# Turning every second tile of the first pass with VectorE and a DRAM round trip instead of TensorE

## The reference

```
x = x + s4(cond(x, style))         # first pass
x = x + ffn(cond2(x, style))       # second pass
cond:  four modulated 1-D convolutions (same, upsample, same, downsample), no nonlinearity between them
s4:    y = causal convolution of each row with one 1024-long kernel K, plus D * u
ffn:   base linear 1024 -> 1024, plus a routed LoRA (8 experts, top 2, rank 16)
```

## Time and profile before

| | |
|---|---|
| median of 3 runs | 1319.42 us (1319.32 to 1320.6) |
| profiled execution: time, span | 1320.42 us, 1318.6 us |
| TensorE busy | 1276.2 us (97%) |
| VectorE, GpSimd, ScalarE busy | 1043.9 (79%), 916.6 (70%), 842.3 us (64%) |
| DMA moved | 158.23 MB, mean 120 GB/s |
| first pass, turns 1 to 32 | 68.38 to 590.88 us of the span |
| a first-pass turn without extra work | 15.5 us |

### The profile page before, as it was taken

One profiled execution on the slowest core, in us unless ns is written; L12 is line 12 of the kernel. 1 busy time (PEld: TensorE's weight loads), 2 busy tenths in 40 slices (PEclk: granted clock), 3 DMA queues, 4 the chain that ended last, 5 costly groups with the idle time before them and its releaser, 6 DMA issues.

```text
span 1318.6 us, 23280 instructions
## 1 busy us (share of the span) xinstructions
PE 1276.2 (97%) x8214; PEld 1220.5 (93%) x8214; DVE 1043.9 (79%) x2311; ACT 842.3 (64%) x1772; POOL 916.6 (70%) x730
## 2 busy tenths in 40 slices
PE   3789999999999999999999999999999999999999
PEld 3578899999899999999999999999999999999998
DVE  7777878777877777877878888788887878788872
ACT  4577777778777877776556555565656565565640
POOL 6458888666666777666768766676776767676752
PEclk9789999999999999999999999999999999999999
DMA  3234455445544554455443342433425252433433
GB/s 131 78 92 138 124 142 150 133 122 146 134 135 135 137 136 138 131 151 147 85 130 105 101 134 79 126 109 111 124 83 152 79 149 86 131 104 114 121 85 90
DMA packets 86278, 158.23 MB, mean 120 GB/s; under 512 B 26634, under 2 KB 48403, under 8 KB 86035
## 3 DMA queue, kind: packets, MB, share of 16 engines
q1 hardware_dynamic: 84898, 154.79, 41.8%
q10 hardware_dynamic: 1264, 1.96, 0.5%
HBM read 93.79 MB, written 33.56 MB: 97 GB/s over the span
## 4 chain that ended last, share of the span: by engine, by line
PE 87%; DVE 5%; POOL 4%; ACT 2%; issue 1%; DMA 1%; SPq 0%; POOLq 0%; DVEq 0%; ACTq 0%
PE psum L1905 28%; PE psum L1907 28%; PE psum L1906 27%; PE psum L2036 2%; POOL xs_l L964 1%; DMA w3T<-in_w_dram 1%; POOL vs_l L959 1%; POOL as_l L993 1%; PE psum L289 1%; DVE vm_l L1635 0%; POOL vbuf L943 0%; POOL vbuf L939 0%; DVE turned L1685 0%; DVE a_l L1662 0%; PE psum L2203 0%
## 5 line engine op out<-in xcount | busy, mean ns | idle before, releaser
L1905 PE MATMUL psum<-wt_h,u_h 128*128 128x386 f32 (+1 forms) x760 | 261.2, 344 | 0.0
L1907 PE MATMUL psum<-wt_h,u_l 128*128 128x386 f32 (+1 forms) x760 | 258.3, 340 | 0.0
L1906 PE MATMUL psum<-wt_l,u_h 128*128 128x386 f32 (+1 forms) x760 | 258.0, 340 | 0.0
L939 POOL TENSOR_TENSOR vbuf<-vbuf 128x512 f32<-128x512 f32 x64 | 97.7, 1526 | 170.4 <-ACT vbuf L1260 170.4
L1685 DVE STREAM_TRANSPOSE turned<-vbuf 32x256 f32<-32x256 f32 x480 | 208.9, 435 | 7.9 <-ACT vbuf L1246 0.7
L953 POOL TENSOR_TENSOR vm_f<-vm_f 128x512 f32<-128x512 f32 x64 | 82.8, 1293 | 120.8 <-DVE vm_l L1635 120.4
L1253 ACT ACTIVATE vbuf<-psum,tabs 128x512 f32<-128x512 f32 x128 | 105.2, 822 | 93.2 <-PE psum L1907 89.6
L1905 PE MATMUL psum<-a_h,vm_h 128*128 128x256 f32 x512 | 148.4, 290 | 3.2 <-ACT vbuf L1253 3.0
L1906 PE MATMUL psum<-a_l,vm_h 128*128 128x256 f32 x512 | 146.0, 285 | 0.0
L1907 PE MATMUL psum<-a_h,vm_l 128*128 128x256 f32 x512 | 145.8, 285 | 0.0
L1905 PEld LDWEIGHTS psum<-wt_h,u_h 128*128 128x128 f32 x760 | 143.7, 189 | 0.5
(11 more groups left out here) (336 smaller groups left out, 4187.5 us busy)
## 6 DMA issues: line engine op xcount, KB each, us to landing
vm_f<-vv SPq DMA_DIRECT2D x256, 112.0 KB, 4.3
xin<-in_x_ph_dram SPq DMA_DIRECT2D x32, 512.0 KB, 5.0
xr<-in_x_row_dram SPq DMA_DIRECT2D x32, 512.0 KB, 3.9
x1d<-xr SPq DMA_DIRECT2D x64, 256.0 KB, 3.3
xin<-x1d SPq DMA_DIRECT2D x32, 512.0 KB, 4.0
xr<-x1d SPq DMA_DIRECT2D x64, 256.0 KB, 5.2
xo<-in_b_base_dram SPq DMA_DIRECT2D x32, 512.0 KB, 5.6
out_dram<-xo SPq DMA_DIRECT2D x31, 512.0 KB, 2.8
```

Source lines behind the costliest of these rows:

```text
L939: G.tensor_tensor(v3[:, :, 1:H:2], v3[:, :, 1:H:2], by_odd, ALU.subtract).then_inc(v3_odd, 1)
L1905: nc.tensor.matmul(to, stat_h, mov_h, start=first_ and n == 0, stop=False, skip_group_check=True)
L1906: nc.tensor.matmul(to, stat_h, mov_l, start=False, stop=False, skip_group_check=True)
L1907: ins = nc.tensor.matmul(to, stat_l, mov_h, start=False, stop=end, skip_group_check=True)
```

## The change

It concerns the tiles g = 3, 5, ... 31 of the first pass ("spun" tiles, 15 of them).

- TensorE no longer turns them. VectorE does two 32x32-block transposes of the finished tile into `xo` (`spin`, after `layer0(i+1)` and before `composed2(i+1)` in turn i), having written the corrected end columns itself. SyncE, at the head of its list of turn i+1, stores `xo` to a DRAM tensor `spin`, waits until it has landed and until `s4` of the tile before is done, and loads it back with four DMAs so that the blocks change places.
- In turn i+1 ScalarE makes `u_h` from `xo` in two halves after `third_evacuated` and before `layer0`, and `s_h` after `layer0`. VectorE makes the neighbour sums and the low part of one half before its `layer0`. GpSimd makes the low part of the other half and `s_l`, after `combined` (`landed`).
- In turn i+1 TensorE runs `step1` before `s4`. `s4` of a spun tile waits for both halves of the low part before its tail, and its order is tail, phases, both. `layer0(i+1)` doesn't wait for the turned tile there.
- The residual additions follow the new order, with `composed1` between them. The high part of the first weights `y1_h` moves in these turns from VectorE to ScalarE.

```diff
+            def spin(g):                                   # SyncE
+                sp.wait_ge(tr_done, at(g))
+                sp.dma_start(sh.spin, xo[:, :]).then_inc(spin_out, 16)
+                sp.wait_ge(spin_out, 16 * spins(g))
+                sp.wait_ge(s4_done, at(g - 1))
+                for t in range(4):
+                    src = bass.AP(tensor=sh.spin.tensor, offset=sh.spin.offset + 2 * P * t, ap=[[L, 32], [32 * L, 4], [1, 2 * P]])
+                    sp.dma_start(xo[32 * t:32 * t + 32, :].rearrange("p (f n) -> p f n", f=4), src).then_inc(u_land, 16)
             def body(i):
+                if spun(i - 1):
+                    spin(i - 1)
                 if first(i - 2):
...
+            def landed(g):                                 # GpSimd
+                pool.wait_ge(u_hi, at(g))
+                G.tensor_tensor(u_spun[1][:, 1], u_runs[:, 1], u_spun[0][:, 1].bitcast(F32), ALU.subtract).then_inc(odd_lo, 1)
+                pool.wait_ge(s_hi, at(g))
+                G.tensor_tensor(s_spun[1], s_runs, s_spun[0].bitcast(F32), ALU.subtract).then_inc(s_lo, 1)
...
-                if first(i - 1):
+                if first(i - 1) and not spun(i - 1):
                     sum_low(i - 1)
                 if here(i):
                     combined(i)
+                if spun(i - 1):
+                    landed(i - 1)
...
+            def landed(g):                                 # ScalarE
+                act.wait_ge(u_land, 64 * spins(g))
+                for q in range(2):
+                    ins = A(u_spun[0][:, q], u_runs[:, q], ACT.Copy)
+                ins.then_inc(u_hi, 1)
...
+                elif spun(i - 1):
+                    if here(i):
+                        act.wait_ge(tr_done, at(i - 1))
+                        pair_evacuated(i, 0)
+                    if here(i + 2):
+                        scaled1(i + 2)
...
+            def landed(g):                                 # VectorE
+                ve.wait_ge(u_land, 64 * spins(g))
+                ve.wait_ge(s_lo, at(g - 1))
+                V.tensor_tensor(s_runs, u_runs[:, 0, :, 0:6], u_runs[:, 1, :, 0:6], ALU.add).then_inc(sum_ready, 1)
+                ve.wait_ge(u_hi, at(g))
+                V.tensor_tensor(u_spun[1][:, 0], u_runs[:, 0], u_spun[0][:, 0].bitcast(F32), ALU.subtract).then_inc(u_lo, 1)
+            def spin(g):                                   # VectorE
+                c, t = place(g)
+                ve.wait_ge(v3_val, at(g))
...
+                V.tensor_copy(v3[:, :, 0:H:H - 1], sh.vfix[:, c, batches(t), :]).then_inc(v3_fix, 1)
+                ve.wait_ge(v3_fix, at(g))
+                ve.wait_ge(s_lo, at(g - 1))
+                for b in range(2):
+                    ins = V.transpose(view(xo, 32 * b, (256, 4), (64, 4), (1, 32)),
+                                      v3[:, b, :].rearrange("p (n t x) -> p t n x", t=4, x=32))
+                ins.then_inc(tr_done, 1)
...
                 if here(i + 1):
                     layer0(i + 1)
+                if spun(i):
+                    spin(i)
...
                     residual_begin(i - 1)
-                    if crowded(i) and here(i + 2):
+                    if (crowded(i) or spun(i - 1)) and here(i + 2):
                         composed1(i + 2)
                     residual_end(i - 1)
...
+                if spun(g):                                # TensorE, s4
+                    pe.wait_ge(u_lo, at(g))
+                    pe.wait_ge(odd_lo, spins(g))
+                product(ps_tail, [(*s4_rows(g, 7 - r), sh.tail_h[:, r, :, :].rearrange("p q n -> p (q n)"),
...
+                for to, stat, tb in ((*phases, both) if spun(g) else (both, *phases)):
+                    if stat is None:
+                        pe.wait_ge(s_lo, at(g))
...
+                if spun(i - 1) and here(i + 2):
+                    pe.wait_ge(blur, at(i + 1))
+                    step1(i + 2)
                 if first(i - 1):
...
-                if here(i) and not by_blocks(i):
+                if here(i) and not by_blocks(i) and not spun(i):
                     if here(i + 1):
                         pe.wait_ge(a_lo, at(i + 1, 2, 1))
                         pe.wait_ge(as_sum, at(i + 1))
```

More of the change, by code:

```diff
@@ L158, in build @@
         sh.kpad = nc.dram_tensor("kpad", [1, PAD + L], F32, kind="Internal").ap()
+        sh.spin = nc.dram_tensor("spin", [P, L], F32, kind="Internal").ap()
         sh.x1d = nc.dram_tensor("x1d", [TILES, P, 2, H], F32, kind="Internal").ap()
@@ L438, in program @@
     u_l = sb("u_l", [P, KT, 2, C], FR)
+    u_spun = [view(t, 0, (512, 2), (32, 2), (64, 8), (1, 32)) for t in (u_h, u_l)]
     vm_f = sb("vm_f", [P, 2, 2, 2, P])
@@ L459, in program @@
     s_h = sb("s_h", [P, 3, P], FR)
+    with ExitStack() as landing:
+        s_in = sb("s_in", [P, 3 * P], F32, landing)
     s_l = sb("s_l", [P, 3, P], FR)
@@ L471, in program @@
     hw = sb("hw", [P, ER])
+    s_spun = [view(t, 0, (32, 2), (64, 6), (1, 32)) for t in (s_h, s_l)]
+    s_runs = view(s_in, 0, (32, 2), (64, 6), (1, 32))
+    u_runs = view(xo, 0, (512, 2), (256, 2), (32, 8), (1, 32))
     hwT_h, hwT_l = s_h[:, 0, :], s_h[:, 1, :]
@@ L576, in program @@
     in_scaled = sem("in_scaled")
+    spin_out, u_land, odd_lo = sem("spin_out"), sem("u_land"), sem("odd_lo")
     ms_sum, ms_hi, ms_lo = sem("ms_sum"), sem("ms_hi"), sem("ms_lo")
@@ L695, in nth, with spun, spins @@
         return n * (g - HALVED) + i + 1
+    def spun(g):
+        return here(g) and SPUN <= g < TILES and (g - SPUN) % 2 == 0
+    def spins(g):
+        return max(0, (g - SPUN) // 2 + 1)
     def turned_f(g):
@@ L820, in body @@
                 if turn_is(i, TILES):
+                    sp.wait_ge(u_lo, TILES)
+                    sp.wait_ge(odd_lo, spins(TILES - 1))
                     sp.wait_ge(s_lo, TILES)
@@ L1602, in scaled1 @@
                 c, t = place(g)
-                if g > 2:
+                if g > 2 and not spun(g - 3):
                     if t == 0:
@@ L1838, in body @@
             def body(i):
-                if here(i - 1):
+                if here(i - 1) and not spun(i - 1):
                     turned(i - 1)
-                if first(i - 1):
+                if first(i - 1) and not spun(i - 1):
                     even_and_odd(i - 1)
@@ L1886, in body @@
                     lora(place(i - 1)[1])
-                if here(i + 2) and not (first(i - 1) and crowded(i)):
+                if here(i + 2) and not (first(i - 1) and (crowded(i) or spun(i - 1))):
                     composed1(i + 2)
@@ L2040, in rows, with s4_rows @@
                 return (u_h[:, k, :, :].rearrange("p b c -> p (b c)"), u_l[:, k, :, :].rearrange("p b c -> p (b c)"))
+            def s4_rows(g, k):
+                if spun(g):
+                    return [view(t, 512 * (k % 2) + P * (k // 2), (1, P)) for t in (u_h, u_l)]
+                return rows(k)
             def s4(g, i):
@@ L2047, in s4 @@
                     pe.wait_ge(toep_lo, 1)
-                product(ps_tail, [(*rows(7 - r), sh.tail_h[:, r, :, :].rearrange("p q n -> p (q n)"),
+                if spun(g):
+                    pe.wait_ge(u_lo, at(g))
+                    pe.wait_ge(odd_lo, spins(g))
+                product(ps_tail, [(*s4_rows(g, 7 - r), sh.tail_h[:, r, :, :].rearrange("p q n -> p (q n)"),
                                    sh.tail_l[:, r, :, :].rearrange("p q n -> p (q n)")) for r in range(2)], True, True)\
                     .then_inc(s4_tail, 1)
-                pe.wait_ge(s_lo, at(g))
                 if g == 0:
                     pe.wait_ge(toep_lo, 3)
-                for to, done, tb, stat in ((ps_p, s4_both, 0, None), (ps_q[:, 0, :], None, 1, 0), (ps_q[:, 1, :], s4_done, 2, 1)):
+                both = (ps_p, None, 0)
+                phases = ((ps_q[:, 0, :], 0, 1), (ps_q[:, 1, :], 1, 2))
+                for to, stat, tb in ((*phases, both) if spun(g) else (both, *phases)):
+                    if stat is None:
+                        pe.wait_ge(s_lo, at(g))
                     if stat == 1:
@@ L2057, in s4 @@
                     for j in range(3):
-                        st = (s_h[:, j, :], s_l[:, j, :]) if stat is None else rows(2 * j + stat)
+                        st = (s_h[:, j, :], s_l[:, j, :]) if stat is None else s4_rows(g, 2 * j + stat)
                         n = H - P * j
                         ins = product(to[:, P * j:H], [(*st, toep_h[:, tb, 0:n], toep_l[:, tb, 0:n])], j == 0, j == 2)
-                    if done is not None:
-                        ins.then_inc(done, 1)
+                    if stat == 1:
+                        ins.then_inc(s4_both if spun(g) else s4_done, 1)
+                    if stat is None:
+                        ins.then_inc(s4_done if spun(g) else s4_both, 1)
             def ffn(n, js=range(KT)):
@@ L2162, in body @@
                 if here(i + 1):
-                    if here(i - 1) and not by_blocks(i - 1):
+                    if here(i - 1) and not by_blocks(i - 1) and not spun(i - 1):
```

(2 more changed lines are left out.)

21 lines of the change are left out of this document (20 added, 1 removed).

## The result

The changed kernel takes 1403.61 us (median of 4 runs, 1402.75 to 1403.92), against 1319.37 (1317.98 to 1320.6) for the kernel before: a ratio of 1.0638 with a 95% interval of 1.0619 to 1.0656. It is 84.2 us slower. The profiled execution took 1403.92 us, with a span of 1402.1. The forecast was 1399, range 1367 to 1432.

What follows compares the result with a forecast made beforehand. TensorE, busy 97% of the span, was taken to set the first pass's time. Per pair -0.8 + 1.75 + 3.45 = +4.4 us, +66 for 15 pairs, -4 for small products, +18 for the clock: +80, 1399 us, range 1367 to 1432.

Steps and rivals of the forecast that it cites:

- The transposes, -0.8 per pair: TensorE loses eight transposes in the odd turn of each of 15 pairs of turns: 0.8 us gained.
- `spin` delays `c_l`: +1.75 per pair: VectorE's `spin` makes `c_l` late, so the next turn's `step2` waits 1.75 us (1.2 to 2.1).
- GpSimd's low part: +3.45 per pair: Odd half's low part stands behind `combined` on GpSimd, so `s4` of the spun tile waits 3.45 us (3.2 to 3.8).
- the six turns named: Turns 10, 12, 14, 20, 28, 30: small products between `third` and `s4` fill part of the gap, -4 us.
- The clock: +1.2 per B turn, 18 in all: TensorE's clock falls in most turns with the long waits: 1.2 us each (0 to 3), +18 us.
- B turn: Second turn of each of 15 pairs, where `s4` of the tile turned by VectorE runs; forecast 20.7 us or more.
- Rival 1: Both TensorE waits come, at `step2` and `s4`, but the clock stays up: 1381 us; chance 0.22.
- What was set at nothing: Costs taken as zero: SyncE's DRAM round trip, `s_l`, `vs_l`, and moved work of VectorE and ScalarE in idle time before `layer0`.
- rival 2: DRAM round trip ends last, +2 us per pair, 1429 us; chance 0.12, shared with two clock falls a turn.
- rival 3: Faster: TensorE's waits stay below the 0.8 us gained; if all fits, 12 us gained, 1307 us; chance 0.06.
- the 0.6 us of room before `step2`: VectorE's chain ends with `c_l` at 16.39 us, and the next turn's `step2` takes it at 16.99.
- Its signs: Expected in the profile: first-pass TensorE busy about 85%, 15 waits each near 1.7 and 3.4 us, lower clock after long waits.

Runs made afterwards that it cites:

- e2: Changed kernel with GpSimd making the low part of the odd half ahead of `combined`, `s_l` still behind it: 1376.16 us, ratio 1.0429.
- e1: Changed kernel with the moved `step1` issued six times instead of once, filling the wait before `s4` with useless products: 1387.16 us, ratio 1.0513.
- e5: Changed kernel with SyncE storing `xo` to DRAM and awaiting it twice before the loads: 1404.25 us, ratio 1.0648.
- e12: Changed kernel with the high part of the first weights moved back to VectorE: 1407.47 us over two runs.
- e6: Kernel before with seven of the eight TensorE transposes of the 15 tiles left out and nothing in their place: 1317.48 us, ratio 0.9988.
- e3: Changed kernel with VectorE making the low part of the odd half too, behind the even half, instead of GpSimd: 1365.03 us, ratio 1.0345.
- e7: Changed kernel with `composed1` before the last residual addition in odd turns, ScalarE's `u_h`, `s_h` and GpSimd's low parts brought forward: 1351.95 us, ratio 1.0248.
- e9: As e8, with ScalarE evacuating `pair(i, 0)` before copying the turned tile in odd turns: 1337.22 us, ratio 1.0131.
- e8: As e7, with `step1` before `s4` in odd turns as well and `composed1` made still earlier: 1332.39 us, ratio 1.011.

## Why the prediction was right

The forecast was 80 us on top, 84.2 were measured, and its terms came out as follows.

- **The transposes, -0.8 per pair.** A turn without extra work lasts 14.68 us, as forecast.
- **`spin` delays `c_l`: +1.75 per pair.** 1.38 in the undisturbed turn, 15.9 us in all instead of 26. The two transposes took 1.31 us, not 1.44, and the copy of the end columns 0.16, not 0.2. In turns 6, 14, 18 and 26 `composed1` stood earlier anyway and the wait was 0.2 us or less; these turns the sum had not set apart.
- **GpSimd's low part: +3.45 per pair.** 3.66, and 49.7 us in all. Small products filled part of it in the six turns named, in which the waits were 2.29 to 3.26 us; that is 5 us in sum where 4 were forecast. `e2` shows that the place in GpSimd's queue made 3.06 us of it.
- **The clock: +1.2 per B turn, 18 in all.** About 22 by `e1`. Rival 1, that it stays up, is refuted. Its rule was that of the Trainium skill, "TensorE: Matmul & The Clock Gate", Part 1: a window without matmuls brings the clock down. The trace agrees in that the falls come late in the long wait or just behind it, and never behind the 1.38 us one. But the length of the wait doesn't sort the turns. In 12 of the 15 B turns the clock fell; in turns 10, 12 and 14, with waits of 3.26, 2.83 and 2.43 us, it did not, and in 28 and 30, with 2.98 and 2.29, it did, for as long as in turn 24. Turn 6 has a fall of its own behind the 2.00 us wait for `xr` at its start; in `e1_filled` the same wait, 1.99 us, brought none. What sorts them is open. The forecast had read the rule as leaving the 3.45 us wait safe for the most part, and here the row of the kernel before was the better guide.
- **What was set at nothing.** The round trip is hidden (`e5`; 2.6 and 2.9 us for its DMAs), so the round trip of rival 2 is refuted. Its other half, two falls of the clock in a turn, happened once, in turn 6. `s_l` is hidden, and the move of the weights' high part is worth nothing (`e12`, in its waits). Not nothing were three waits for VectorE (`xr`, `ssq`, `xmid`), 6.1 us in all against 0.2 before, which no term had.

The sum, measured: -12.0 for the transposes, +15.3 and +49.7 for the waits, +22 for the clock, +5.9 for VectorE's other waits and -1.8 for fewer waits for `vs_l`, together +79.1. Some 5 us of the 84.4 are left. In `e1_filled`, at full clock, turn 24 lasts 20.96 us and its parts are 15.48 + 1.38 + 3.55 + 0.18 = 20.59; 0.37 us per B turn stay over, in steps of about 0.1 at each wait. The bracket before `step2` says 1.38 us, but `step2` starts 1.48 us late (2.99 us into the turn instead of 1.51), and its first product then takes 0.41 us where the earlier trace rows has 0.31. In 15 turns the 0.37 are 5.6 us.

Its signs were met too: over the first pass TensorE's busy share is 87% where about 85 was expected, and the B turns last 20.0 to 23.6 us.

So the total came out closer than its terms, and that was luck. `c_l` was priced 10 us too high in sum; the clock, VectorE's other waits and the restarts were 15 too low.

**The side statement that failed** is rival 3's gain of 15 x 0.8 = 12 us if both waits were gone. With no extra work on any engine, `e6` gains 1.6 us. TensorE's waits before, the 3.4 us of the earlier trace rows and 0.8 more, read as if it alone set the time, and the forecast wrote that what is taken off it counts; they don't say how soon the next engine follows. The forecast had noted the 0.6 us of room before `step2` for VectorE, but didn't take it off the gain. The expectations of `e3` and `e7` to `e9` repeated the mistake, crediting nearly the full wait, and that of `e2` allowed for one new wait only.

## What to carry to other kernels

Where all engines are about two thirds busy or more, as here, the gain of relieving the busiest is bounded by the slack of the next chain, so measure it first by leaving the work out, as `e6` does. An operation that feeds the next stage belongs in its engine's queue by its due time: placed behind 4.5 us of other work it made a 3.7 us wait. A wait of that length on TensorE cost more than itself here, by about 1.5 us of slow clock; where it can't be removed, useless products in it can give the clock back, as in `e1_filled`.

## What the runs showed of the hardware

- **Useless matmuls made the kernel faster.** 53 us of them gave back 16.4 (`e1`). In turn 24 the clock was at 1.2 GHz for some 3.4 us (0.87, 0.50 and 0.77 in three stretches of 2 us), in turns 4 and 20 for 6.8 us. Which turns fall, and for how long, differs between the traces of the changed kernel and of `e12` at equal waits, and `e12`'s two runs lie 8 us apart (clock 0.969 and 0.977).
- **VectorE and GpSimd hold each other up where both read two SBUF inputs.** `vm_l` took 1.25 us for two at 498.05 and 3.14 at 513.14, beside GpSimd's `u_l` and `s_l` (513.04 to 515.74). VectorE's `u_l` at 509.45 took 1.15 us beside `combined` and ended at 510.60; GpSimd's next pass, begun at 510.13, took 1.37 us, where in `e8`, at 464.86, the same pass took 1.04. As `u_l` stands behind this pass in GpSimd's list, the 0.33 us is part of the 3.66 us wait. The Trainium skill, "SBUF — State Buffer", section "SBUF: two separate sides", says that the pair of ports which the two engines share is locked for a whole instruction and the other engine waits; the trace agrees: the pass of line 971 ends at 510.05, VectorE's `u_l` 0.55 us later (one of the two that take 1.25 alone is 0.63), and GpSimd's next ends 0.90 after that.

In `e8_first_weights_early` a small operation of VectorE that takes 0.60 us for two in the changed kernel stood beside a long one of GpSimd. First its line in VectorE's timeline, then that of GpSimd's operation; it ends 0.43 us after GpSimd's 459.27:

```profile
457.43 2.27 DVE L1676 SCALAR_TENSOR_TENSOR y_l<-x1w,tabs,y_h 128x128 fp32r<-128x128 f32 x2
```

```profile
457.08 2.19 POOL L1003 TENSOR_TENSOR xs_l<-xin,xs_h 128x1024 fp32r<-128x1024 f32 x1
```
